# Relation stage of a four-layer graph network: splitting TensorE's products into alternating runs, and a softmax reciprocal into two halves one turn apart

## The reference

```python
proj = jnp.einsum('ni,rio->nro', nfeat, relation_weight)   # 10 relations, 64 x 64 each
t_r = proj[src, etype]
h_r = proj[dst, etype]
att = jnp.sum(t_r * jnp.tanh(h_r + efeat), axis=-1)
seg_max = jax.ops.segment_max(att, dst, num_segments=n)
ex = jnp.exp(att - seg_max[dst])
seg_sum = jax.ops.segment_sum(ex, dst, num_segments=n)
a = ex / seg_sum[dst]
h_nb = jax.ops.segment_sum(nfeat[src] * a[:, None], dst, num_segments=n)
out = leaky_relu((nfeat + h_nb) @ res_fc_w.T, 0.01) + leaky_relu(nfeat * h_nb @ res_fc2_w.T, 0.01)
```

## Time and profile before

| | |
|---|---|
| median of 3 runs | 6235.68 us (6197.13 to 6236.36) |
| profiled execution, its own time | 6214.3 us |
| its span in the trace | 6212.5 us |
| relation stage in the trace | some 3528 to 4968 us |
| busy in the whole span | PE 5134.0, DVE 3278.3, ACT 1898.0, POOL 2770.6 us |
| mean granted clock of TensorE | 0.827 of full speed |

### The profile page before, as it was taken

How to read it: one execution, slowest core, us unless ns; L and a number is a source line. 1 busy time by engine, 2 the same in 40 slices (tenths; PEclk the granted TensorE clock), 3 DMA queues, 4 the chain that set the end, 5 groups by cost and what they waited for, 6 DMA issues and landing times. The chain is left out here.

```text
span 6212.5 us, 80161 instructions
## 1 busy us (share of the span) xinstructions
PE 5134.0 (83%) x25341; PEld 3285.1 (53%) x25341; DVE 3278.3 (53%) x6838; ACT 1898.0 (31%) x3531; POOL 2770.6 (45%) x2859
## 2 busy tenths in 40 slices
PE   6899988888889999727888789999999877777776
PEld 1266666666667676604555545555555534444443
DVE  9755555555544444526555467777777622222222
ACT  0055554333333333301111114444444311111111
POOL 0144443545544444463542153433332056666665
PEclk9899998899989999956565598888888677777777
DMA  1177776666754454323332243333333122222221
GB/s 31 37 214 218 221 221 190 165 167 174 177 147 136 129 138 133 102 54 82 90 87 73 58 101 82 91 87 90 86 86 78 29 67 54 53 46 52 54 54 24
DMA packets 1124519, 649.11 MB, mean 104 GB/s; under 512 B 907542, under 2 KB 940589, under 8 KB 1124104
## 3 DMA queue, kind: packets, MB, share of 16 engines
q1 hardware_dynamic: 1036296, 555.84, 33.0%
q0 software_dynamic: 87808, 88.16, 7.1%
HBM read 384.69 MB, written 261.63 MB: 104 GB/s over the span
## 5 line engine op out<-in xcount | busy, mean ns | idle before, releaser
L1047 POOL DMA_INDIRECT o_rows<-in_x_dram,dst_idx x392 | 370.0, 944 | 661.8 <-POOLq L347 265.9
L1488 POOL DMA_INDIRECT b_rows<-h_table,slot_idx x392 | 369.8, 943 | 440.9 <-DVE n_res L1021 318.9
L2591 DVE TENSOR_TENSOR_SCAN m_both<-m_keep,m_both,m_rows_t 128x512 f32<-128x512 bf16 x97 | 124.2, 1280 | 815.0 <-remote 458.1
L2464 POOL DMA_INDIRECT out_dram<-s_res,put_out x392 | 390.4, 996 | 352.6 <-DVE s_res L1241 223.9
L1931 POOL DMA_INDIRECT t_got<-x_table,slot_idx x392 | 370.8, 946 | 383.9 <-DVE t_rows L2041 239.7
L1305 POOL DMA_INDIRECT a_got<-node_table,src_idx x392 | 372.0, 949 | 368.5 <-DVE n_res L1021 214.2
L1201 ACT ACTIVATE s_square<-s_sum_t 128x256 f32<-128x256 f32 x392 | 149.2, 381 | 1232.6 <-remote 580.3
L2245 PE MATMUL r_source_t<-r_masked,rel_pair 64*128 64x512 f32 x980 | 523.0, 684 | 0.0
L2247 PE MATMUL r_own_t<-r_masked,rel_pair 64*128 64x512 f32 x980 | 522.8, 684 | 0.0
L1007 DVE TENSOR_REDUCE n_power<-n_square 128x8 f32<-128x512 f32 x294 | 200.9, 683 | 604.9 <-ACT n_square L982 312.0
L2146 POOL DMA_INDIRECT r_got<-x_table,slot_idx x392 | 382.4, 976 | 297.8 <-POOLq L1920 183.0
(11 more groups left out here) (390 smaller groups left out, 13082.2 us busy)
## 6 DMA issues: line engine op xcount, KB each, us to landing
x_table<-n_res SPq DMA_DIRECT2D x196, 256.0 KB
n_rows<-x_table SPq DMA_DIRECT2D x196, 256.0 KB
x_table<-s_res SPq DMA_DIRECT2D x294, 128.0 KB
node_table<-n_wide SPq DMA_DIRECT2D x98, 272.0 KB
h_table<-n_conv SPq DMA_DIRECT2D x98, 256.0 KB
x_table<-s_res SPq DMA_DIRECT2D x98, 256.0 KB
r_feats<-in_edge_attr_dram SPq DMA_DIRECT2D x390, 64.0 KB
n_rows<-in_x_dram SPq DMA_DIRECT2D x97, 256.0 KB
```

Of the source, the lines that this page charges most:

```text
L1047: nc.gpsimd.indirect_dma_start(out=rows[:, n % 4, t, :], out_offset=None, in_=x, in_offset=bass.IndirectOffsetOnAxis(ap=dst_idx[:, n * TIL ...
L1488: nc.gpsimd.indirect_dma_start(out=rows[:, n % 4, t, 0:D], out_offset=None, in_=h_table, in_offset=bass.IndirectOffsetOnAxis(ap=slot_idx[: ...
L2464: nc.gpsimd.indirect_dma_start(out=out, out_offset=bass.IndirectOffsetOnAxis(ap=put_out[:, n * TILES + t:n * TILES + t + 1], axis=0), in_= ...
```

## The change

Three edits. In PE's list, `project` and `add_up` are cut into parts and alternate: `add_up` of tiles 0 and 1, the products of pair 0, `add_up` of tiles 2 and 3, pair 1, the small products of the softmax, the features of tiles 0 and 1, pair 2, the features of tiles 2 and 3, pairs 3 and 4. `r_own_t` is now started by pair 0 and no longer by the features, so the waits for `bent_made` and `picked_made` stand ahead of pair 0. In the `Softmax` class the reciprocal is done in two halves: `start_shares` (clamp and first half) and `share_out` (second half and the rest). In the relation stage these are turns 8 and 9, and what follows moves by one turn (`turn_shares`, `keep_shares`, `store_betas`, `X`, with it the two rings); in the attention stage both stand in the same turn. The lists of ACT and POOL stay. Although the change's name speaks of the scan first and the join early, `sum_up` and `join` hold the places in the lists that they had.

```diff
-            nc.vector.reciprocal(self.share[:, :], self.total[:, :]).then_inc(self.inverted[c], 1)
+            half = EDGE_BLOCK // 2
+            nc.vector.reciprocal(self.share[:, 0:half], self.total[:, 0:half]).then_inc(self.half_inverted[c], 1)
+
+        def share_out(self, dve, c):
+            half = EDGE_BLOCK // 2
+            nc.vector.reciprocal(self.share[:, half:EDGE_BLOCK], self.total[:, half:EDGE_BLOCK]).then_inc(self.inverted[c], 1)
...
-        X = CH + 8
+        X = CH + 9
...
+                    def project_pairs(k):
+                        def at_turn(n):
+                            if k == 0:
+                                if n >= 1:
+                                    pe.wait_ge(bent_made[n - 1], bent_made.done(n - 1))
+                                    pe.wait_ge(picked_made[n - 1], picked_made.done(n - 1))
                             pe.wait_ge(masks_made[n], masks_made.part(n, k + 1))
                             nc.tensor.matmul(source_t[:, :], rel_pair[0:D, k, :], masked[0:D, n % 2, k, :], start=(k == 0),
                                              stop=(k == PAIRS - 1), skip_group_check=True)
-                            last = nc.tensor.matmul(own_t[:, :], rel_pair[D:P, k, :], masked[D:P, n % 2, k, :], start=False,
+                            last = nc.tensor.matmul(own_t[:, :], rel_pair[D:P, k, :], masked[D:P, n % 2, k, :], start=(k == 0),
                                                     stop=(k == PAIRS - 1), skip_group_check=True)
...
-                               soft.after(6, soft.turn_ends, pe), soft.after(8, soft.turn_sums, pe), soft.after(9, turn_shares, pe),
-                               (add_up, X + 4, BLOCKS), soft.after(6, soft.turn_peaks, pe), soft.after(8, soft.turn_totals, pe),
-                               (project, 2, BLOCKS))
+                               soft.after(6, soft.turn_ends, pe), soft.after(8, soft.turn_sums, pe), soft.after(10, turn_shares, pe),
+                               add_up((0, 1)), project_pairs(0), add_up((2, 3)), project_pairs(1),
+                               soft.after(6, soft.turn_peaks, pe), soft.after(8, soft.turn_totals, pe),
+                               add_feats((0, 1)), project_pairs(2), add_feats((2, 3)), project_pairs(3), project_pairs(4))
...
-                               soft.after(8, soft.enter_totals, dve), soft.after(8, soft.sum_all, dve), soft.after(8, soft.share_out, dve))
+                               soft.after(8, soft.enter_totals, dve), soft.after(8, soft.sum_all, dve), soft.after(8, soft.start_shares, dve), soft.after(9, soft.share_out, dve))
```

More of the change, by code:

```diff
@@ L1654, in __init__ @@
             self.summed, self.fades_copied, self.totals_run, self.total_entered = (Step(vector, k) for k in (11, 12, 14, 15))
-            self.totalled, self.guarded, self.inverted, self.shared = (Step(vector, k) for k in (16, 17, 18, 19))
-            self.left, self.betas_made, self.shares_kept = (Step(vector, k) for k in (20, 21, 22))
+            self.totalled, self.guarded, self.half_inverted, self.inverted, self.shared = (Step(vector, k) for k in (16, 17, 18, 19, 20))
+            self.left, self.betas_made, self.shares_kept = (Step(vector, k) for k in (21, 22, 23))
             self.ends_turned, self.peak_back, self.sums_turned, self.total_back, self.shares_turned = (Step(tensor, k) for k in (1, 2, 3, 4, 5))
@@ L2092, in _ @@
                                soft.after(9, soft.run_totals, dve), soft.after(10, soft.enter_totals, dve),
-                               soft.after(10, soft.sum_all, dve), soft.after(10, soft.share_out, dve))
+                               soft.after(10, soft.sum_all, dve), soft.after(10, soft.start_shares, dve), soft.after(10, soft.share_out, dve))
             sig.end_phase()
@@ L2207, in store @@
                         norm.store(sp, n, of_slots(x3_table, block_of(n)))
-                    over_turns((load, 0, BLOCKS), (load_feats, 0, BLOCKS), (load_soft, 1, BLOCKS), soft.after(9, soft.store_betas, sp),
+                    over_turns((load, 0, BLOCKS), (load_feats, 0, BLOCKS), (load_soft, 1, BLOCKS), soft.after(10, soft.store_betas, sp),
                                (load_betas, X, BLOCKS), (store, X + 5, BLOCKS))
@@ L2246, in project, with add_feats, at_turn @@
                                              stop=(k == PAIRS - 1), skip_group_check=True)
-                            last = nc.tensor.matmul(own_t[:, :], rel_pair[D:P, k, :], masked[D:P, n % 2, k, :], start=False,
+                            last = nc.tensor.matmul(own_t[:, :], rel_pair[D:P, k, :], masked[D:P, n % 2, k, :], start=(k == 0),
                                                     stop=(k == PAIRS - 1), skip_group_check=True)
-                        last.then_inc(projected[n], 1)
+                            if k == PAIRS - 1:
+                                last.then_inc(projected[n], 1)
+                        return at_turn, 2, BLOCKS
+                    def add_feats(part):
+                        def at_turn(n):
+                            pe.wait_ge(feats_in[n], feats_in.done(n))
+                            for t in part:
+                                nc.tensor.matmul(own_t[:, t * P:(t + 1) * P], feats[:, n % 3, t].rearrange("p k d -> p (k d)"), ident[:, :],
+                                                 start=False, stop=False, skip_group_check=True)
+                        return at_turn, 2, BLOCKS
                     def match(n):
@@ L2268, in write, with add_up, at_turn @@
                                          skip_group_check=True).then_inc(written[m], 1)
[L2270 to L2280, removed]
+                    def add_up(part):
+                        def at_turn(m):
+                            pe.wait_ge(leaked[m], leaked.done(m))
+                            if m >= 1:
+                                pe.wait_ge(norm.ready[m - 1], norm.ready.done(m - 1))
+                            to = norm.sum_t[0]
+                            for t in part:
+                                k = slice(t * P, (t + 1) * P)
+                                nc.tensor.matmul(to[:, t, :], leaky[:, m % 2, k], cen2[:, 0:D], start=(t == 0), stop=False, skip_group_check=True)
+                                last = nc.tensor.matmul(to[:, t, :], scan[D:P, m % SCANS, k], cen2[D:P, 0:D], start=False, stop=True,
+                                                        skip_group_check=True)
+                            if part[-1] == TILES - 1:
+                                last.then_inc(norm.summed[m], 1)
+                        return at_turn, X + 4, BLOCKS
                     def turn_shares(eng, k):
@@ L2417, in _ @@
                                soft.after(6, soft.run_peaks, dve), soft.after(8, soft.copy_fades, dve),
[L2418 removed]
+                               soft.after(8, soft.run_totals, dve), soft.after(10, keep_shares, dve), (weigh, X, BLOCKS), (mask, 1, BLOCKS),
                                (powers, X + 4, BLOCKS), (leak, X + 3, BLOCKS),
```

5 lines of the change are left out of this document (3 added, 2 removed).

## The result

| | before | changed |
|---|---|---|
| median of 20 runs | 6200.15 us (6176.63 to 6238.43) | 6257.49 us (6221.67 to 6284.28) |
| ratio, 95% interval | | 1.0081 (1.0062 to 1.0100) |
| profiled execution, its span | 6212.5 us | 6240.5 us |
| relation stage, first to last scan of DVE | 1395.5 us | 1449.8 us |

The change made the kernel 0.8% slower, where 0.8% faster was forecast. In the profiled executions the relation stage holds the whole loss: its scans run from 3537.95 to 4933.49 before and from 3514.01 to 4963.76 after, 54 us more; the two spans differ by less (28 us), since in the changed kernel's execution the stages ahead ended 24 us earlier.

A forecast was written before the change was run, and what follows sets the result against it. PE, partly at half clock, bounds the kernel, with DVE second in turn 8. Loaded turns give -62 us, costs elsewhere +11: -51, so 6163 from the profiled 6214 or 6185 by the median; 6175 named, range 6130 to 6215.

The forecast's parts named there:

- The step that failed: SP's queue: `store_betas` and `load_betas` keep their order behind the betas, so nothing moves against anything; no cost.
- rival 2: PE's clock does not answer to the order, one 1.61 us stretch in each turn: +31 us, say 6254; chance 0.2.
- a turn 7 or 9 over 14 us: Sign of a wrong forecast in the relation stage: it would put the bound on ACT's or DVE's chain.
- The alternation and the clock: PE's ordinary turns: shorter light parts, 2.1 us before the first long product, keep full clock and save 1.61 a turn.
- Its cycle of 88.55 us: Seven loaded turns of the relation stage, before adding 1.6 for one half-clock stretch; result 90.2 against 95.6 before.
- The seams: PE's loaded turns: each run of long products costs 0.19 us at its ends; three more runs, 0.57 a turn.
- The first rival: PE's seams are hidden under other work, ordinary turn 11.7: -88 us in all, say 6138; chance 0.2.
- The 0.10 for the wait on the tanh: PE's pair 0 waits for ACT's tanh of the block before: 0.1 us a turn, bounds 0 and 0.3.
- DVE's and ACT's chain: Softmax turns 6 to 9: sums end 1.15 us later, giving turns of 12.4, 13.05, 13.3 and 12.9.
- One half-clock stretch a cycle, 1.6: PE idles 0.6 to 1.0 us more ahead of the join after late turns 7 to 9, leaving one 1.6 us stretch.
- The count of 14 stretches of 3.3 us: Kernel before, fourteen loaded turns: a quarter of the time, 46 us, at half clock in about 14 stretches.
- The third rival: PE's spread-out light parts keep the clock down longer, two half-clock stretches a turn: +150 us, near 6380; chance 0.1.

The follow-up runs named there:

- the kernel with the later load: Changed kernel (four runs of long products) with SP's load of the softmax rows moved from lag 1 to lag 3: ratio 0.9919, 6171 against 6234 us.
- four runs and the exponentials first: Changed kernel with the load at lag 3, plus turn 7's exponentials ahead of `squares` and DVE's first sums ahead of `powers`: ratio 0.9929 to the kernel before.
- three runs: Changed kernel with the load at lag 3 and the features in one piece, so long products run in 2, 2 and 6 steps: ratio 0.9911 to the kernel before.
- three runs and the exponentials first: Long products in 2, 2 and 6, load at lag 3, turn 7's exponentials ahead of `squares`, first sums ahead of `powers`: ratio 0.9859, 6085 against 6172 us.

## Why the prediction was wrong

The forecast was -51 us; the change measured +57 (medians), +54 in the relation stage of the trace. The absolute forecast, 6175 us, also started too high: the 20 runs of the kernel before have a median of 6200 us, where the three shown ahead of it had 6236. By the prediction's own steps:

- **The step that failed** is "`store_betas` still stands one turn behind the DVE turn that makes the betas, and `load_betas` just behind it, so nothing moves against anything on SP". It followed the two steps whose lags had been looked at, and not the third one on SP that waits for `betas_made`: `soft.load`, whose lag the change does not touch. Since the betas moved by a turn and the load did not, the load now meets them. Taking the wait away is worth 0.9919 against 1.0081; putting it alone into the kernel before costs 1.0%. No rival named it either, not even the slower one. That rival 2 had said 6254, close to the measured 6257, is luck: its mechanism, a clock that does not answer to the order, is out. The sign "a turn 7 or 9 over 14 us" did come, but not for the reason given with it: DVE's own work in turn 9 ended after 12.85 us, and the rest was SP.
- **What it cost.** In turns 9 and 10 of the cycle shown, (16.85 + 19.05) - (12.9 + 12.3) = 10.7 us, so the wait of 4.0 us is less than half of it. The rest is the clock: PE idled for 4.99 us ahead of the join and ran turn 10 at 0.57. Over the 77 turns the two kernels differ by 1093.1 - 986.5 = 106.6 us, 9.7 a cycle.
- **The alternation and the clock** were right: loaded turns outside 8 to 10 stand at 1.00. In the kernel with the later load a whole cycle does, and 77 turns of that kernel take 66 us less than before; the prediction's 81 loaded turns gave 62. Its cycle of 88.55 us is 88.37 there.
- **The seams** were 0.57 + 0.10 for a turn of 12.3; measured 12.26, but not by these two terms alone. The first rival's free seams are out. The 0.10 for the wait on the tanh did not come: over its 980 products into `r_source_t` the changed kernel waits 1.4 us for `r_bent`. In its place stands what the prediction put at nothing, cutting the run of features, 1.28 against 1.08 us; the sums, 2.81 us in one piece before, give back some 0.1. So in filling turns the cost is 9.47 - 8.94 = 0.53 and not 0.38, which had counted the long runs alone.
- **DVE's and ACT's chain**: turns 6 to 9 forecast 12.4, 13.05, 13.3, 12.9; measured 12.52, 12.90, 13.05, 12.85 of work. Half a reciprocal is 1.73 us, taken at 1.7.
- **"One half-clock stretch a cycle, 1.6"** was mis-sized. Behind a short idle time a fall in turn 10 costs 4.7 us with the later load (17.26 against 12.6), and behind the long one of the changed kernel 4.5 to 6.4. With the later load it is rarer than assumed, three cycles in eleven (1.3 us a cycle), and so the sum came out right there by two errors; in the changed kernel turn 10 fell in every cycle. The count of 14 stretches of 3.3 us was off too: the 5.50 us stretch of the earlier trace rows stands at 0.50 from end to end. In those 14 turns the falls last 3.4 or 6.8 us, and a turn with the longer one, turn 8 apart, takes 15.0 to 15.2.
- **The third rival**, that the alternation keeps the clock down longer, is wrong for the ordinary turns, which do not fall. It is right in part for the turns that do: behind a short idle time a fall in the alternating order lasts most often 10.2 us, against 3.4 or 6.8. Its condition, that the clock comes back only behind a long run, did not hold, and a run of eight long products did not shorten the turn.

That the wait makes the loss and that the two parts help each other is shown. What sets whether a turn behind a short idle time falls, and why its fall then lasts so long, stays open: 3 cycles in 11 with four runs, 9 with four runs and the exponentials first, 8 and 7 with three runs.

## What to carry to other kernels

When a step is moved by a turn, list every wait on what it produces, on every queue, and ask for each whether it is now met in the same turn; a wait of a rarely needed load blocks everything behind it on an in-order queue, here the factors for the next scan. Price an idle time of PE by what its clock does afterwards: 4 us of waiting took 10.7 us in the cycle shown and 9.7 on average. And test the parts of a change alone and together, since here either one looked doubtful without the other. The version with the load moved is about 0.8% faster than the kernel before and, by the ratios, 1.6% faster than the change; with three runs and the exponentials first it is 1.4% faster than before.

## What the runs showed of the hardware

- The clock fell in turns in which PE was busy 98% of the time (12.92 of 13.21 us) and idle for no more than 0.29 us ahead of the join, in a part of 4.6 us without a 512-column product. In the changed kernel, where that part is 2.1 us in an ordinary turn, turns 5, 6 and 11 stayed at 2.4 GHz.
- In the kernel before half clock lasted 3.4 or 6.8 us behind idle times up to 1.5 us; in the alternating orders it lasted 10.2 us, with PE busy throughout, in most falls behind 0.9 to 1.6 us.
- Behind 4.3 to 5.1 us of idle time PE ran for another 9.5 to 14.4 us at 1.2 GHz although it was busy, in both orders.
- Each run of 512-column products costs 0.19 us at its two ends, 0.53 and 0.52 us instead of 0.43 from start to start; cutting the run of features in two costs another 0.20.
- A reciprocal of 7x512 numbers takes DVE 3.34 us and one of 7x256 1.73; an elementwise product of the same 7x512 shape takes 0.68.
